# Newton steps as split fp32r products of [F|V], with the convolution groups set one by one between the steps

## The reference

```
x = x + conv3x3(gn(x), w0) + b0            # stage A
x = x + newton_schulz(gn(x), 5)            # stage B
x = x + circular_conv3x3(gn(x), w2)        # stage C (written with FFTs)
x = x + masked_conv3x3(gn(x), K)           # stage D: last row and column are zero
```

## Time and profile before

| | |
|---|---|
| median of three runs | 698.35 us |
| profiled execution | 701.13 us, span 699.5 us |
| granted TensorE clock, mean | 0.974 of full speed |
| TensorE products busy | 623.8 us (89%) |
| VectorE busy | 448.1 us (64%) |
| ScalarE busy | 348.9 us (50%) |
| GpSimd busy | 120.7 us (17%) |
| moved by DMA | 60.85 MB |

### The profile page before, as it was taken

One profiled execution on the slowest core, in us unless ns is written; L12 is line 12 of the kernel. 1 busy time (PEld: TensorE's weight loads), 2 busy tenths in 40 slices (PEclk: granted clock), 3 DMA queues, 4 the chain that ended last, 5 costly groups with the idle time before them and its releaser, 6 DMA issues.

```text
span 699.5 us, 13159 instructions
## 1 busy us (share of the span) xinstructions
PE 623.8 (89%) x4200; PEld 533.8 (76%) x4200; DVE 448.1 (64%) x1454; ACT 348.9 (50%) x617; POOL 120.7 (17%) x235
## 2 busy tenths in 40 slices
PE   0596894999999999899989999899999999989756
PEld 0365894899879897698869897698879897888544
DVE  3868238766885857766876657856785648356560
ACT  0252552655457265454557374554567265546432
POOL 5024022120213021120212002120210021000202
PEclk9998997999999999999999999999999999999888
DMA  5131043252226314252235314262134214400432
GB/s 153 49 93 42 28 66 114 61 138 58 92 79 146 94 37 126 79 150 60 70 91 128 108 32 133 79 154 62 63 96 99 68 39 131 112 31 32 128 99 60
DMA packets 82837, 60.85 MB, mean 87 GB/s; under 512 B 8238, under 2 KB 75982, under 8 KB 81870
## 3 DMA queue, kind: packets, MB, share of 16 engines
q1 hardware_dynamic: 78558, 54.80, 28.8%
q0 software_dynamic: 4224, 5.43, 3.2%
HBM read 23.46 MB, written 16.91 MB: 58 GB/s over the span
## 4 chain that ended last, share of the span: by engine, by line
PE 69%; DVE 10%; DMA 7%; SPq 6%; issue 5%; ACT 2%; DVEq 0%; POOL 0%; ACTq 0%
PE conv_ps L612 31%; PE V_ps L763 18%; PE R_ps L753 16%; DMA win_C<-rows_dram 4%; SPq L315 3%; DVE x L959 2%; PE R_ps L702 2%; DMA rows_dram<-x 2%; DVE d_A L500 2%; SPq L282 1%; SPq L268 1%; PE V_ps L709 1%; DVE sums L902 1%; DMA x<-out_C 1%; ACT d_C L528 1%
## 5 line engine op out<-in xcount | busy, mean ns | idle before, releaser
L763 PE MATMUL V_ps<-V,R 128*128 128x128 f32 x1280 | 168.9, 276 | 0.0
L763 PEld LDWEIGHTS V_ps<-V,R 128*128 128x128 f32 x1280 | 156.0, 193 | 0.1
L753 PE MATMUL R_ps<-R 128*128 128x128 f32 x1024 | 137.4, 278 | 6.6 <-DVE R L939 6.6
L753 PEld LDWEIGHTS R_ps<-R 128*128 128x128 f32 x1024 | 125.9, 194 | 7.2 <-DVE R L939 7.2
L612 PE MATMUL conv_ps<-d_C,w_C 128*96 128x512 f32 (+1 forms) x486 | 115.7, 393 | 16.4 <-DVE d_C L500 6.4
L612 PEld LDWEIGHTS conv_ps<-d_C,w_C 128*96 128x96 f32 x486 | 76.0, 167 | 48.3 <-DVE d_C L500 11.2
L612 PE MATMUL conv_ps<-d_A,w_D 128*96 128x512 f32 (+1 forms) x432 | 99.6, 386 | 5.5 <-DVE w_D L493 3.9
L830 ACT ACTIVATE R<-R_ps 128x512 f32<-128x512 f32 x128 | 76.0, 594 | 43.0 <-PE R_ps L753 42.3
L832 ACT ACTIVATE V<-V_ps 128x512 f32<-128x512 f32 x128 | 76.3, 596 | 35.6 <-PE V_ps L763 35.6
L612 PE MATMUL conv_ps<-d_A,w_A 128*96 128x512 f32 (+1 forms) x378 | 88.3, 389 | 4.0 <-DVE d_A L500 4.0
L612 PEld LDWEIGHTS conv_ps<-d_A,w_D 128*96 128x96 f32 x432 | 66.8, 164 | 31.1 <-DVE w_D L493 4.0
(11 more groups left out here) (170 smaller groups left out, 644.7 us busy)
## 6 DMA issues: line engine op xcount, KB each, us to landing
win_C<-rows_dram SPq DMA_DIRECT2D x40, 256.0 KB, 4.0
rows_dram<-x SPq DMA_DIRECT2D x32, 256.0 KB
y<-out_D SPq DMA_DIRECT2D x160, 48.0 KB
win_D<-out_C SPq DMA_DIRECT2D x7, 1056.0 KB, 6.8
x<-out_A SPq DMA_DIRECT2D x139, 48.0 KB
win_A<-x SPq DMA_DIRECT2D x84, 64.0 KB
win_A<-x POOLq DMA_DIRECT2D x56, 64.0 KB, 2.8
win_D<-out_C SPq DMA_DIRECT2D x14, 160.0 KB, 5.9
```

Of the source, the lines that this page charges most:

```text
L753: ins = pe.matmul(R_ps[s][:, m, :], Rk[:, m, :], Rk[:, m, :], start=True, stop=True)
L763: ins = pe.matmul(V_ps[s][:, m, :], Rk[:, m, :], V[ch][:, m, :], start=False, stop=True, skip_group_check=True)
```

## The change

Stage B is written anew, and the order of the work with it.

- **Algebra.** A matrix pair [F|V] of 256 columns lies in PSUM (`z`, two tensors of two banks) and is only accumulated into. Slot j = 0 puts in the transpose of DS (DN times the negative scale) and the product DN^T DS. Slots 1 to 4 each add F times [F|V], with F and V scaled by powers of two (`ROOT`), as three fp32r products of 256 columns per matrix (high x high, high x low, low x high). Slot 5 adds the last F V as a plain fp32 product of 128 columns. Between two slots of the same chunk ScalarE writes the high part `zh` and VectorE the low part `zl`, each 128 x 1024 elements.
- **DS** is computed by GpSimd (`pool_DS`), 128 x 512 per chunk. R, its copies and `dve_R0` are gone. The norms of batch i+1 are found in cycle i, by transposes into a bank of their own (`pe_norm_T`) and `dve_abs`.
- **x2** is x1 copied by one DMA of 1 MB (`keep_x1` on SyncE), to which VectorE adds the scaled V, one instruction per pair of channels (256 columns).
- **Order.** A cycle has 24 slots (2 rounds x 6 x 2 chunks). Behind every slot but each fourth stands one convolution group: D of batch i-2 in slots 1 to 7, C of batch i-1 in slots 9 to 15, A of batch i+2 in slots 17 to 23. D's statistics are now taken from C's output instead of from D's windows. The lists of all engines follow the slots.
- **SyncE** issues all window loads of x (22 a batch), and its order is: windows of x2 of batch i-1, the copy of x1 to x2, the wait for it, the 22 rows into x1 for batch i+1, y of batch i-2, half of the stores of x2, windows of D, windows of x of batch i+3, the other stores.
- The loop holds cycles 2 to 4; behind the last cycle come D of batch 6, and C and D of batch 7.

The core of the diff:

```diff
+        def keep_x1(sp, b):
+            if is_int(b, 0):
+                sp.wait_ge(s_x1, x1_moved(1))
+                sp.wait_ge(s_x1_pool, 16 * n_x1_pool)
+            else:
+                sp.wait_ge(sC_bn, at(2, b, -1))
+            sp.dma_start(x2[:, :, :], x1[:, :, :]).then_inc(s_keep, 16)
...
+        def sp_cycle(sp, i, has_D, has_C, has_A, nxt, load):
+            if has_C:
+                for g in range(NG):
+                    load_x2(sp, i - 1, g)
+            keep_x1(sp, i)
+            if nxt:
+                sp.wait_ge(s_keep, at(16, i, 16))
+                sp.wait_ge(s_DN, at(NCHK, i, NCHK))
+                for g in range(NG):
+                    rows_from_windows(sp, i + 1, g)
+            if has_D:
+                store_y(sp, i - 2)
+            store_x2(sp, i, 0)
+            store_x2(sp, i, 1)
+            if has_C:
+                windows_from_windows(sp, i - 1)
+            if load:
+                for g in range(NG):
+                    load_x(sp, i + 3, g)
+            store_x2(sp, i, 2)
+            store_x2(sp, i, 3)
+            store_x2_edges(sp, i)
...
+        def place(q):
+            return q % 2, q // (2 * SEGS), (q // 2) % SEGS
+        def filler(q):
+            if q % 4 == 0:
+                return None, None
+            return q // 8, 3 * (q % 8 // 4) + q % 4 - 1
+        def pe_slot(pe, b, q):
+            s, r, j = place(q)
+            ch = 2 * r + s
+            if j == 0:
+                pe.wait_ge(s_DS, at(NCHK, b, ch + 1))
+                wait(pe, s_x2, at(NCHK, b, ch - 1 if r else s - 1))
...
+            elif j < STEPS:
+                pe.wait_ge(s_zl[s], at(per_zh, b, (STEPS - 1) * r + j))
+                for m in range(NMAT):
+                    pe.matmul(z[s][:, m, :], zh[s][:, m, 0:128], zh[s][:, m, :], start=False, stop=True,
+                              skip_group_check=True)
+                    pe.matmul(z[s][:, m, :], zh[s][:, m, 0:128], zl[s][:, m, :], start=False, stop=True,
+                              skip_group_check=True)
+                    ins = pe.matmul(z[s][:, m, :], zl[s][:, m, 0:128], zh[s][:, m, :], start=False, stop=True,
+                                    skip_group_check=True)
...
+        def act_slot(act, b, q):
+            s, r, j = place(q)
+            if j == STEPS:
+                return
+            act.wait_ge(s_z[s], at(per_z, b, n_z(r, j)))
+            if j < STEPS - 1:
+                act.activation(zh[s][:, :, :], z[s][:, :, :], ACT.Copy, scale=ROOT[j]).then_inc(s_zh[s], 1)
+            else:
+                act.activation(z4[s][:, :, :], z[s][:, :, :], ACT.Copy, scale=ROOT[j]).then_inc(s_z4[s], 1)
...
+        def dve_slot(dve, b, q):
+            s, r, j = place(q)
+            if j < STEPS - 1:
+                dve.wait_ge(s_zh[s], at(per_zh, b, (STEPS - 1) * r + j + 1))
+                dve.scalar_tensor_tensor(zl[s][:, :, :], z[s][:, :, :], ROOT[j], zh[s][:, :, :].bitcast(f32),
+                                         ALU.mult, ALU.subtract).then_inc(s_zl[s], 1)
+            elif j == STEPS:
+                dve_x2(dve, b, 2 * r + s, s, r)
...
+        def dve_cycle(dve, i, has_D, has_C, has_A, nxt, load):
+            for q in range(SLOTS):
+                dve_slot(dve, i, q)
+                if has_D and q in (2, 3, 5, 6):
+                    low_parts(dve, cD, i - 2, {2: 2, 3: 3, 5: 4, 6: 5}[q])
...
+                if has_C and q == 1:
+                    row_stats_1(dve, x2, stC, sC_bn, 1)
+                if has_C and q == 2:
+                    link_C = dve_rows_C_mean(dve, i - 1)
+                if has_C and q == 3:
+                    row_stats_3(dve, link_C, sC_sum, sC_ve, M_ROWC, tC, i - 1)
...
+                if has_A and q == 3:
+                    win_stats_1(dve, cA, i + 2, 0)
+                if has_C and q == 3:
+                    dve_rows_C_scale(dve, link_C, i - 1)
+                if has_C and q == 5:
+                    dve_rows_C_weights(dve, link_C, i - 1)
+                if nxt and q == 5:
+                    dve.wait_ge(s_x1, x1_moved(i + 2))
+                    row_stats_1(dve, x1, stB, sB_bn, 0)
+                if has_C and q == 6:
+                    low_parts(dve, cC, i - 1, 0)
+                if nxt and q == 6:
+                    row_stats_1(dve, x1, stB, sB_bn, 1)
...
+                if has_C and q == 23:
+                    win_stats_4(dve, cD, i - 1)
+                    win_weights(dve, cD, i - 1)
+                    low_parts(dve, cD, i - 1, 0)
+                    low_parts(dve, cD, i - 1, 1)
```

More of the change, by code:

```diff
@@ L84, in wait @@
     eng.wait_ge(sem, value)
+KAPPA = [2.0 ** (k - 1) for k in range(STEPS)]
+ROOT = [k ** 0.5 for k in KAPPA]
+SEGS = STEPS + 1
+SLOTS = 2 * ROUNDS * SEGS
 def build(nc, x, w0, b0, w2, w3, consts, y, rows_dram):
@@ L708, in pe_transposes, with pe_norm_T @@
+        def pe_norm_T(pe, b, ch, out=None):
+            pe.wait_ge(s_DN, at(NCHK, b, ch + 1))
+            if out is None:
+                out = spare_ps
+                wait(pe, s_Ta, at(NCHK, b, ch))
             for m in range(NMAT):
@@ new lines, in pe_norm_spread, with pe_filler @@
+        def pe_norm_spread(pe, b):
+            pe.wait_ge(s_dg, at(1, b, 1))
+            pe.matmul(misc_ps[:, M_NB:M_NB + 2 * C], ones_all[0:2 * C, :], diag[:, :],
+                      start=True, stop=True).then_inc(s_nB, 1)
+        def pe_filler(pe, i, q, has_D, has_C, has_A):
+            part, g = filler(q)
+            if part == 0 and has_D:
+                conv_group(pe, cD, i - 2, g, (cA, i + 1) if has_A or not is_int(i, B - 1) else (cC, i - 2))
+            if part == 1 and has_C:
+                conv_group(pe, cC, i - 1, g, (cD, i - 2) if has_D else (cA, i + 1))
+            if part == 2 and has_A:
+                conv_group(pe, cA, i + 2, g, (cC, i - 1) if has_C else (cA, 1))
@@ new lines, in dve_x2 @@
+        def dve_x2(dve, b, ch, s, r):
+            dve.wait_ge(s_z[s], at(per_z, b, n_z(r, STEPS)))
+            if ch == 0:
+                dve.wait_ge(s_keep, at(16, b, 16))
+            for a in range(NMAT // GC):
+                g = ch * NMAT // GC + a
+                cs = slice(GC * g, GC * (g + 1))
+                ins = dve.scalar_tensor_tensor(x2[:, cs, :], z[s][:, GC * a:GC * (a + 1), 128:256], sx[:, g:g + 1],
+                                               x2[:, cs, :], ALU.mult, ALU.add)
+            ins.then_inc(s_x2, 1)
@@ L1095, in dve_end @@
+            dve_rows_C_scale(dve, link_C, i)
+            dve_rows_C_weights(dve, link_C, i)
+            for g in range(NG):
+                low_parts(dve, cC, i, g)
+            win_stats_1(dve, cD, i, 0, 1, 2)
+            win_stats_2(dve, cD, i)
+            win_stats_3(dve, cD, i)
+            win_stats_4(dve, cD, i)
+            win_weights(dve, cD, i)
             for g in range(NG):
```

819 lines of the change are left out of this document (367 added, 452 removed).

## The result

The changed kernel takes **797.43 us** (median of four runs, 796.59 to 799.33) against 697.87 for the kernel before (four runs). The ratio is 1.143, 95% interval 1.139 to 1.147. The forecast was 797, in the range 718 to 830.

A forecast was written before the change was run, and what follows sets the result against it. TensorE bounds the kernel before; in the changed one VectorE's 12 us wait for x1's rows makes 91.5 us cycles. 133 + 457.5 + 80 + 63.5 + 59.5 = 793.5, plus 5 for loop heads, adjusted to 797 us; range 718 to 830.

The forecast's parts named there:

- the wait, its place and its chain: VectorE waits in slot 5 for x1's rows, behind copy and row issues: 12 us a cycle; X is a batch's x2 end.
- the fourth rival: Worse: TensorE idles 14 us a cycle, partly at 1.2 GHz; low parts 1.49 us, fp32r products 0.2: over 830 us; chance 8%.
- the rest of the sum: Span terms: first x2 end 133, cycles 1 to 5 457.5, cycle 6 80, cycle 7 63.5, tail 59.5 us.
- the 5 us that I had set aside for loop heads: VectorE loses 3.04 us to issue at a loop round's head; 5 us added for two rounds, span 798.5.
- from the span to the median: Profiled run 1.6 us over its span, 800 us; profiled run before 0.4% over its median, so 797 us.
- its three terms: Range 770 to 828: copy 3 to 8 us (-19 to +6), low part 1.1 to 1.49 (-12 to +14), handovers (-15 to +10).
- The low part: VectorE's low part of 1024 columns from PSUM: 1.28 us each, sixteen a cycle, 20.5 us.
- my row's 6.8: Copy of x1 to x2 on SyncE, priced from another 1056 KB SBUF-to-SBUF DMA: 6.8 us to landing, between 3 and 8.
- what sets the 54 us behind the wait: After the rows land, VectorE's remaining work sets the pace: 54 us plus 3.5 us of idle, cycle 91.5 us.
- VectorE's 75 us plus 5 of handovers would be next: Without the stall for rows, VectorE would set the steady cycle at 80 us.
- TensorE at 74 us a cycle and VectorE at 75: Steady cycle: TensorE about 74 us after saving 2.4; VectorE 70.3 busy, 75 with handovers, so VectorE passes TensorE.
- the products: TensorE's middle slots: twelve fp32r products of 256 columns at 0.130 us, 1.57 us a slot, 25.1 a cycle.

The follow-up runs named there:

- run 1: Changed kernel with the copy of x1 to x2 left out for batches 1 to 7: 758.7 us, ratio 1.086.
- run 6: Changed kernel without the copy for batches 1 to 7 and with eight of 22 row DMAs issued by GpSimd: 734.8 us, ratio 1.052.
- run 2: Changed kernel, complete, with the copy of x1 to x2 issued ahead of the windows of x2: 780.7 us, ratio 1.118.
- run 3: Changed kernel, complete, with eight of the 22 row DMAs issued by GpSimd: 785.1 us, ratio 1.124.
- 4 both: Changed kernel, complete, with the copy ahead of the windows of x2 and eight row DMAs on GpSimd: 765.3 us, ratio 1.097.
- 5 no low parts: Changed kernel without VectorE's low parts zl (set to zero once), TensorE's products and the wait for rows kept: 772.3 us, ratio 1.105.
- run 7: Changed kernel without the copy for batches 1 to 7, eight row DMAs on GpSimd, and no low parts zl: 703.1 us, ratio 1.005.
- the square above: Profiled spans with and without VectorE's low parts: rows late 795.3 and 771.6 us, rows in time 732.4 and 703.4 us.
- runs 5 and 9: First: 5 no low parts. Second: 4 both, with the low parts of convolution C formed on GpSimd instead of VectorE, 764.0 us, ratio 1.090.
- run 11: Changed kernel, transfers unchanged, with VectorE's statistics of the next x1 three slots later: 824.6 us, ratio 1.178.
- run 8: 4 both, with VectorE's statistics of the next x1 and what hangs on them one slot later: 757.4 us, ratio 1.081.

## Why the prediction was right, and where it was not

**Right: the wait, its place and its chain.** Copy, its landing, 22 issues one by one, VectorE's statistics, D's low part, TensorE. Forecast: rows landed at X+34, VectorE there at X+22, 12 us of wait. Measured: statistics start at X+34.2, VectorE free at X+23.7, 10.6 us. Inside this sum two errors cancel, and that is luck: the copy starts at X+9.9 instead of X+7.8, and lands in 5.3 us (median) instead of 6.8. The wait costs nearly what it measures where it was taken away: against the changed kernel it fell by 40.2 us in run 1 and 60.8 in run 6, and the span by 36.2 and 62.9. Where issues were only moved it was worth less, down to 16.3 us of span for 26.3 of wait in run 2. The clock fell in the stop and was still low just behind it, as the fourth rival had it, but that rival's other conditions did not come.

**Right in size: the rest of the sum.** The first end of x2, X(0), 130.9 (forecast 133); cycles 1 to 5 453.5 (457.5); cycle 6 84.3 (80); cycle 7 64.5 (63.5); tail 62.1 (59.5). These sum to the whole span of 795.3, so the 5 us that I had set aside for loop heads were not there besides. That the median came within half a microsecond of 797 is luck: the terms are off by -2, -4, +4, +1 and +2.6 us, the 5 us were not needed, and from the span to the median I had taken off 1.5 us where 2.1 came on. In the range, the lower ends of its three terms sum to 751, not to 770; the upper ones give the 828. VectorE's busy time in a cycle is 69.1 us (70.3). The low part takes 1.22 us; I had drawn 1.28 from rows. By the page "VectorE: DVE Perf Modes" of the Trainium skill (the section on the TRN2 errata) the estimate was 1.19: for this shape it was the nearer one, while for the 342 ns instruction the rows stood above its rule. By the page "DMA: Bandwidth & Descriptors" of the Trainium skill (the section on the anatomy of one DMA, whose figures are for DMAs that GpSimd issues) the estimate for the copy, which SyncE issues, was 4.4 us; it takes 5.3, nearer to that than to my row's 6.8.

**Wrong: what sets the 54 us behind the wait.** The step was "After the wait VectorE still has 75 - 21 = 54 us of work, with some 3.5 us of idle", and the step after it, that without the stall VectorE's 75 us plus 5 of handovers would be next. The numbers fit (57.6 us behind the wait; cycles of 78.0 to 81.6 in run 6), the cause does not. One steady cycle of each run, in us:

| run | X to statistics | statistics to next X | wait over the span |
|---|---|---|---|
| changed kernel | 34.2 | 57.6 | 70.5 |
| 1 no copy | 27.2 | 57.7 | 30.3 |
| 2 copy early | 30.5 | 57.7 | 44.2 |
| 3 rows split | 30.9 | 58.0 | 56.0 |
| 4 both | 26.2 | 56.7 | 26.8 |
| 6 no wait | 25.1 | 56.5 | 9.7 |
| 5 no low parts | 34.4 | 54.4 | 97.0 |
| 7 no wait, no low parts | 23.0 | 53.5 | 32.3 |

The second column hardly depends on what VectorE has to do: with 9.75 us less VectorE work in it, it is 3 us shorter. It is the time that TensorE needs from that point: 50 to 52 us of work, and the end of its stop. The low parts cost the few places where a product waits for one (24 to 29 us over the span, by the square above). I had TensorE at 74 us a cycle and VectorE at 75, and gave the pace to the larger; with both that close, the engine whose idle time is smallest behind the wait was the one to name. In the second half of the changed kernel's cycle (363.4 to 402.8) TensorE is busy 36.9 of 39.4 us. No run took work from TensorE alone, so that it sets the pace rests on these busy times and on what runs 5 and 9 did not gain.

**Sized wrongly: the products.** I took 0.130 us for an fp32r product of 256 columns; at full clock their pitch is 0.12, so a slot is 1.44 instead of 1.57, and 16 of them save 2.1 us more than forecast. But TensorE's busy time fell by 1.0 us a cycle where I had 2.4: behind the stop a part of the work runs at the 1.2 GHz level. In run 7, whose cycle is at 1.00 throughout, it is 72.3, 3.9 us under the 76.2 of before.

**What would have helped.** The place to read the price of the wait is TensorE: its 11 us stop lies inside SyncE's chain and the 3 us of VectorE's work behind it, so the price of the wait is the stop plus what the clock loses behind it, about 2 us (75.2 busy in the changed kernel, 73.1 in a cycle of run 6).

## What to carry to other kernels

When a step is moved onto one in-order DMA queue behind a wait, add up the queue from the event that frees it to the last landing, and look which engine has an in-order instruction parked at that landing: here that sum (34 us) was the forecast. Then ask which engine is nearest to full behind the wait, not which has the larger total, and take one engine's work out to test it before building on it: 9.75 us less on VectorE bought 3.25. And when a step is moved along an order written by hand, check that each pair of give and take behind it (here absolute sum and transpose) keeps its distance; in run 11 it didn't, and 15 new stops came of it.

## What the runs showed of the hardware

- Issue and landing of a DMA depend on what else is in flight. Six window DMAs of x2 took 3.34 us to issue where no copy was in flight, 5.95 right behind the 1 MB copy (run 2), and the row DMAs took 2.38 us to land from one queue, 5.25 from two (run 3). Edits that only reorder issues or spread them over queues gave a third to a half of what their issue times summed to.
- In TensorE's 11 us without work and just behind them its granted clock was 0.50 (340.0 to 353.5 above); the products of 256 columns ran at a pitch of 0.21 us from 350.9 to 353.3 and of 0.12 behind that.
- Two tiny VectorE operations of D's window statistics take over four times as long while GpSimd computes DS as they do otherwise: 0.80 and 0.96 us against 0.15 and 0.22. Of the eight pairs in the span, six overlap GpSimd's products of DS and are slow (0.70 to 0.80 and 0.96 us), the two at 727.5 and 768.6 have no GpSimd work beside them and are fast. A low part of A that begins beside the same products takes 0.94 us instead of 0.74. The traces show that the two coincide, not why. It costs some 1.4 us of VectorE a cycle, so an operation moved to GpSimd can lengthen those of VectorE beside it.

```profile
300.16 5.01 POOL L1150 TENSOR_TENSOR DS<-DN,scl 128x512 f32<-128x512 f32 x4 [14.82 <-DVE scl L959]
...
303.38 0.80 DVE L445 TENSOR_TENSOR col_D<-mv_D,cst 96x1 f32<-96x1 f32 x1
304.22 0.96 DVE L446 SCALAR_TENSOR_TENSOR col_D<-mv_D,cst,col_D 96x1 f32<-96x1 f32 x1
...
768.57 0.15 DVE L445 TENSOR_TENSOR col_D<-mv_D,cst 96x1 f32<-96x1 f32 x1
768.76 0.22 DVE L446 SCALAR_TENSOR_TENSOR col_D<-mv_D,cst,col_D 96x1 f32<-96x1 f32 x1
```

No version that computes everything came under the kernel before: the best, run 8, stands at 757 us.
